# A two-stream fp32 transformer kernel: feed-forward norms by tokens, contexts of two head groups in one bank, exponents by head pair, new orders

## The chip, the cores and the metric

The kernel runs on one core of a Trainium2 chip, as one program. The metric is the time of an execution on the device, in microseconds. Before the change the median of three runs is 2144.49 us (2142.8 to 2147.58).

## What is computed

Sixteen sequences of 512 tokens and 128 channels, all fp32, each on its own. The reference, with the first norm, the modulation by a condition and the two layers:

```python
# per sequence: x (512, 128), condition c, six vectors from silu(c) @ wmod
# 1 attention with a latent: q = x@W_UQ, k = (x@W_DKV)@W_UK, v = (x@W_DKV)@W_UV
#   16 heads of 8, causal softmax(q k^T / sqrt(8)) v, then @ W_O, gated, added to x
# 2 twice, with weights of layer l:
h = shift_token(x)                 # the second half of the channels comes from the token before
q, k, v = split(h @ wqkv)          # 8 heads of 64
q, k = l2norm(q) * q_scale, l2norm(k) * k_scale
q, k = rotary_xpos(q, k)
o = local_attention(q, k, v)       # windows of 64, each sees itself and the one before
x = x + o @ wo
h = shift_token(x)
h = (h - mean(h)) / sqrt(var(h) + 1e-5) * g + b     # over the 128 channels
a, gate = split(h @ w1 + b1)       # 2 x 341
x = x + (a * gelu(gate)) @ w2 + b2
```

The mean and the variance of the last norm are what the change calls the norm of a feed-forward part.

## The kernel before, in words

Two streams of sequences run beside each other: even sequences in buffers of stream 0, odd ones in those of stream 1, about half a sequence apart. Each sequence is a list of some 190 named steps (`steps()`); a step may have work on TensorE (`pe`), ScalarE (`act`), VectorE (`dve`), GpSimd (`pool`) and SyncE (`sp`, transfers). The order in which each engine takes the steps is written out by hand: `PLACES` is the order inside a stream, `TURNS` says bit by bit which stream is next, `merged()` joins them. No engine deviates from its list, so an instruction that waits holds up everything behind it on its engine.

TensorE's results go to eight banks of PSUM, of 512 fp32 columns each. `FIRST_BANKS` gives each result its bank (some take two); `Banks.take` makes TensorE wait until the readers of the bank's last result are done. `FILLS` puts filler matmuls (constants, 128x512 bf16) into a bank ahead of a result.

The steps of the causal attention: `max` (scores for the row maxima, reduced on VectorE), `rows1` (maxima turned), `score` (scores turned, exponent on ScalarE), `ctx` (context of a group of four heads, 32 small products, L564), `turn` (four transposes, then VectorE divides by the sum), `join`, `out` (product with W_O and the residual; its vector step is L967).

The steps of a layer: `qkv` and `v` (products of 512 columns, L594, L595, L604), the squares on ScalarE (L788), `rotate` on VectorE (cosine product L982, two sine products L989, sum of squares L991) and GpSimd (their sum L1091), `norm` (inverse length, ScalarE; GpSimd scales the keys L1101), `qheads` and `kheads` (transposes). Then by head pair p: `wscore` (scores of 128x1024 into two banks, L636; VectorE's row maxima L1000 and their product with the inverse query lengths L1006), `wexp` (ScalarE, eight calls of 128x128 with own scale, bias and sum, L815), `share` (reciprocals of the sums L1021, GpSimd scales L1108), `pturn` (four transposes per head, copied by VectorE, L1014), `wctx` (context, L658). Then `wout` (product with wo, L667; residual L1026) and the feed-forward part: `center` (product of the centring matrix with the channels-by-tokens h, L491; squares on ScalarE L736), `spread` (product of the averaging matrix with the squares, so that each channel's row holds the variance of each token, L496; logarithm and exponent over 128x512, L739 and L741), `scale` (VectorE multiplies, L928), `hid` (L678, L681, the gelu L832, product L1033), `down` (L687, L1037), `final` (four transposes, the last vector step L1043, and the transfer out). Transposes have one line for all, L430; the filler matmuls are L234.

## Time and profile before

| | |
|---|---|
| median of 3 runs | 2144.49 us |
| profiled execution, first to last instruction | 2140.7 us |
| TensorE busy | 1949.1 us, 91% |
| ScalarE busy | 1607.3 us, 75% |
| VectorE busy | 1559.3 us, 73% |
| GpSimd busy | 862.1 us, 40% |
| instructions | 56,185 |

The busy shares are means over the span. In the view by slices TensorE stands at 9 tenths in all slices but the first three and the last two. Since the streams repeat, one period (from the last vector step of a sequence to that of the next) shows nearly all.

### The profile page before, as it was taken

How to read it: one execution, taken by the hardware profiler on the slowest of the kernel's cores; microseconds unless marked ns; L12 is line 12 of the kernel's file. 1: busy time of each engine (PE TensorE's matmuls, PEld its weight loads, DVE VectorE, ACT ScalarE, POOL GpSimd, SP SyncE). 2: the span in 40 equal slices, each digit the busy share in tenths (PEclk: the TensorE clock that was granted, in tenths of full speed). 3: DMA queues.
4: the chain of work that ended last, by engine and by line, in shares of the span. 5: the costliest groups of instructions: out<-in, count | busy, mean ns of one | idle time of the engine just before them, and what ended most of it. 6: DMA issues, size and time to landing. Idle time of an engine off the chain costs nothing.

```text
span 2140.7 us, 56185 instructions
## 1 busy us (share of the span) xinstructions
PE 1949.1 (91%) x22308; PEld 1117.7 (52%) x22308; DVE 1559.3 (73%) x2671; ACT 1607.3 (75%) x3975; POOL 862.1 (40%) x826
## 2 busy tenths in 40 slices
PE   6789999999999999999999999999999999999987
PEld 3344545555454655545555554655545455554644
DVE  3476787877778777787877778687777877777753
ACT  1567878787887878777787887878688787877755
POOL 2043616245351624526163361625435162452522
PEclk8999999999999999999999999999999999999999
DMA  4110201213030120202112030120203012030100
GB/s 137 29 32 16 61 7 36 41 24 58 7 68 9 39 43 24 58 7 57 21 32 51 24 58 7 38 39 24 58 7 70 13 36 42 24 53 7 36 6 23
DMA packets 63110, 76.19 MB, mean 36 GB/s; under 512 B 10630, under 2 KB 57856, under 8 KB 60800
## 3 DMA queue, kind: packets, MB, share of 16 engines
q1 hardware_dynamic: 62852, 72.60, 16.1%
q8 instruction: 180, 2.95, 0.6%
q14 instruction: 78, 0.64, 0.1%
HBM read 9.14 MB, written 4.19 MB: 6 GB/s over the span
## 4 chain that ended last, share of the span: by engine, by line
PE 56%; ACT 23%; DVE 12%; issue 5%; SPq 2%; DMA 1%; POOL 1%; DVEq 0%; ACTq 0%; POOLq 0%
PE ps L430 10%; ACT pr L815 6%; PE ps L667 5%; PE ps L564 5%; ACT pr L777 5%; PE ps L594 4%; PE ps L595 4%; PE ps L604 4%; PE ps L658 3%; PE ps L449 3%; ACT pr L788 3%; DVE wm L1000 3%; PE ps L678 2%; PE ps L445 2%; PE ps L687 2%
## 5 line engine op out<-in xcount | busy, mean ns | idle before, releaser
L1091 POOL TENSOR_TENSOR pr<-pr 128x1024 f32<-128x1024 f32 x128 | 302.2, 2361 | 739.7 <-DVE pr L989 739.7
L815 ACT ACTIVATE pr<-ps,wb,inv 128x128 f32<-128x128 f32 x768 | 340.8, 481 | 24.6 <-DVE wb L1006 24.2
L777 ACT ACTIVATE pr<-ps 128x1024 f32<-128x1024 f32 x320 | 314.4, 1028 | 42.5 <-PE ps L449 42.0
L1108 POOL TENSOR_TENSOR pr<-pr,shares 128x512 f32<-128x512 f32 x192 | 199.9, 1048 | 314.0 <-DVE shares L1021 314.0
L947 DVE TENSOR_REDUCE nm<-ps 128x2 f32<-128x256 f32 (+2 forms) x384 | 314.5, 861 | 13.0 <-PE ps L449 11.9
L430 PE MATMUL ps<-cf,pr 128*128 128x128 f32 x1792 | 259.7, 282 | 31.1 <-POOL pr L1108 22.5
L430 PEld LDWEIGHTS ps<-cf,pr 128*128 128x128 f32 x1792 | 200.9, 142 | 124.4 <-issue 55.0
L982 DVE TENSOR_TENSOR pr<-ps,rot 128x1024 f32<-128x1024 f32 x128 | 156.2, 1221 | 120.1 <-ACT pr L788 97.7
L788 ACT ACTIVATE pr<-ps 128x1024 f32<-128x1024 f32 x128 | 131.2, 1025 | 104.6 <-PE ps L595 66.2
L445 PE MATMUL ps<-cb 64*64 64x256 bf16 (+1 forms) x2560 | 175.3, 263 | 30.1 <-ACT pr L777 14.4
L1014 DVE COPY pr<-ps 128x512 f32<-128x512 f32 x256 | 170.1, 679 | 15.2 <-PE ps L430 13.7
L815 ACT ACTIVATION_READ_ACCUMULATOR pr<-ps,wb,inv 128x1 f32 x768 | 175.9, 229 | 0.0
L1000 DVE TENSOR_REDUCE wm<-ps 128x8 f32<-128x1024 f32 x128 | 155.6, 1216 | 25.9 <-PE ps L636 25.9
L989 DVE TENSOR_TENSOR pr<-ps,rot 128x512 f32<-128x512 f32 x256 | 163.7, 681 | 0.0
L445 PEld LDWEIGHTS ps<-cb 64*64 64x64 bf16 x2560 | 72.4, 104 | 168.5 <-issue 82.7
L564 PE MATMUL ps<-pr,V 128*16 128x512 f32 (+3 forms) x2048 | 152.4, 439 | 6.3 <-ACT pr L777 6.3
L991 DVE TENSOR_REDUCE scr<-pr 128x16 f32<-128x1024 f32 x128 | 154.8, 1209 | 0.0
L594 PE MATMUL ps<-Wqkv,hs 128*128 128x512 f32 x256 | 137.1, 617 | 7.4 <-ACT pr L777 3.6
L1101 POOL TENSOR_TENSOR pr<-pr,inv 128x512 f32<-128x512 f32 x128 | 133.4, 1042 | 19.3 <-POOL inv L1096 0.4
L636 PE MATMUL ps<-Kf,Q 64*64 64x128 f32 (+1 forms) x4096 | 137.0, 263 | 0.0
L658 PE MATMUL ps<-pr 128*64 128x64 f32 x2048 | 133.4, 229 | 2.1 <-DVE pr L1014 1.9
L636 PEld LDWEIGHTS ps<-Kf,Q 64*64 64x64 f32 x4096 | 129.7, 133 | 4.5
(158 smaller groups left out, 4040.0 us busy)
## 6 DMA issues: line engine op xcount, KB each, us to landing
pr<-V SPq DMA_DIRECT2D x32, 512.0 KB, 4.5
queries<-early SPq DMA_DIRECT2D x224, 64.0 KB
keys<-early SPq DMA_DIRECT2D x224, 64.0 KB
pr<-V SPq DMA_DIRECT2D x32, 384.0 KB, 6.6
xn<-in_L_attn_x SPq DMA_DIRECT2D x16, 256.0 KB, 4.5
out<-hT SPq DMA_DIRECT2D x16, 256.0 KB, 2.2
queries<-mT SPq DMA_DIRECT2D x128, 4.0 KB
Wqkv<-in_L_ffn_wqkv SPq DMA_DIRECT2D x1, 1536.0 KB
```

The lines of the kernel that those rows point to most:

```text
L430: mm = pe.transpose(dst[:, t * P:(t + 1) * P], src(t), ident)
L445: pe.matmul(dst, identb[here, here], mask, start=True, stop=False, skip_group_check=True)
L564: mm = pe.matmul(bank[32 * j:32 * j + 16, kt * P:T], V1[s][:, kt, 4 * g + j, :], pr[s][:, j, OFF[kt]:OFF[kt] + T - kt * P], start=(kt == 0 ...
L594: pe.matmul(bank[:, 0:T], lhs, Wqkv[:, l, 0:T], start=True, stop=True)
L636: mm = pe.matmul(bank[D2 * half:D2 * half + D2, r * T + (t + 1) * P - wd:r * T + (t + 1) * P], Q2[s][rows, p, q0:q0 + D2], K2[s][rows, p, ...
L658: mm = pe.matmul(bank[D2 * r:D2 * r + D2, q0:q0 + D2], val[s][:, t, 2 * p + r, :], PT[s][:, (2 * n + r) % 3, q0:q0 + D2], start=True, stop ...
L777: act.activation(dst, src, ACT.Exp, scale=SC1).then_inc(ex_r[s], 1)
L815: ins = act.activation(P2[s][2 * (p % 3) + r][:, o:o + P], bank[:, r * T + o:r * T + o + P], ACT.Exp, scale=inv[s][:, t, h:h + 1], bias=wb ...
L947: ins = dve.tensor_reduce(nm[s][:, qt, h:h + 2], src[:, :, o:o + (qt + 1) * P], AX_X, ALU.max, negate=True)
L1000: dve.tensor_reduce(dst, src, AX_X, ALU.max, negate=True).then_inc(wm_r[s], 1)
L1091: pool.tensor_tensor(t1[s][t % 3], t1[s][t % 3], t2[s], ALU.add).then_inc(sum_r[s], 1)
L1108: pool.tensor_tensor(part, part, share, ALU.mult).then_inc(part_r[s], 1)
```

## The change

- The norm of a feed-forward part goes by tokens. `center` is four transposes of h in place of the product with the centring matrix; VectorE takes batch statistics of each 128 tokens (mean and variance of 128 channels), `spread` is two calls of ScalarE on 128x4 in place of two on 128x512 and has no product, `scale` multiplies by the inverse deviation and transposes back (four transposes and a copy on ScalarE). W1 is centred ahead, as before.
- `ctx`: the values are laid out 32 columns wide per head, with zeros, so that two groups of four heads add into one bank; one copy and one `turn` serve both.
- `qkv` and `rotate` go by halves, queries and keys, each in one bank. GpSimd now scales the queries too, before their transposes.
- `wexp` is one exponent over 128x1024 per head pair, in place in SBUF: VectorE first subtracts the maxima (from PSUM), and sums the exponents afterwards. The reciprocals go by pair.
- `pturn` is copied by ScalarE in place of VectorE.
- TensorE waits for data before it waits for the bank, but ahead of fillers. Some vector waits that others cover are gone.
- All orders, banks and fillers are new: each stream has a list of its own, the pattern repeats every two sequences; 2,390 banks are given out in place of 2,326, and 308 fillers in place of 161. Between the outputs of sequences 0 and 13 they are 108 (65 before); 104 (56) stand before the first, 96 (40) after that of sequence 13. The first step of sequence 1's causal attention comes after the first head pair of sequence 0's layer 0; before, it came after that layer's first rotations.

The diff, cut to its core (indentation cut too; the orders, turns and banks are strings of digits and lists of step numbers and are left out):

```diff
-    out = [("keep",), ("values",)] + units[0] + [("rows1", 0)] + units[1] + [("rows1", 1)]
+    out = [("stats", 0), ("plain", 0), ("load",), ("proj", 0), ("proj", 1), ("keep",), ("values",)] + units[0] + [("rows1", 0)] + units[1] + [("rows1", 1)]
...
-            if j == 0 and g:
-    out += [("turn", g - 1)]
+            if j == 0 and g == 2:
+    out += [("turn", 0)]
...
-            out += [("qkv", l, t), ("rotate", l, t), ("v", l, t)] * (t < NT) + [("norm", l, t - 1)] * (1 <= t <= NT)
+            out += [("qkv", l, t, 0), ("rotate", l, t, 0), ("qkv", l, t, 1), ("rotate", l, t, 1), ("v", l, t)] * (t < NT) + [("norm", l, t - 1)] * (1 <= t <= NT)
...
-            out += [("wscore", l, p), ("wexp", l, p, 0), ("share", l, p, 0), ("wexp", l, p, 1), ("share", l, p, 1)] * (p < NP2)
+            out += [("wscore", l, p), ("wexp", l, p), ("share", l, p)] * (p < NP2)
...
 FILLS = {
-    2: 2, 7: 20, 17: 7, 69: 10, 70: 3, 74: 2, 77: 6, 103: 1, 187: 4, 188: 1, 332: 4, 333: 1, 477: 4, 478: 1, 622: 4,
-    623: 1, 767: 4, 768: 1, 912: 4, 913: 1, 1057: 4, 1058: 1, 1202: 4, 1203: 1, 1347: 4, 1348: 1, 1492: 4, 1493: 1,
-    1637: 4, 1638: 1, 1782: 4, 1783: 1, 1927: 4, 1928: 1, 2072: 4, 2073: 1, 2217: 4, 2218: 1, 2250: 10, 2254: 2,
-    2257: 1, 2283: 1, 2290: 1, 2292: 3, 2293: 2, 2296: 1, 2304: 2, 2305: 1, 2307: 3, 2308: 1, 2309: 1, 2316: 1,
-    2318: 4, 2325: 1,
+    7: 20, 59: 2, 63: 13, 64: 2, 69: 13, 79: 11, 80: 1, 83: 1, 84: 1, 85: 2, 89: 19, 90: 1, 92: 4, 97: 3, 187: 5,
...
-        for sem, value in dict.fromkeys(self.last[k] + self.last[k + count - 1]):
-            pe.wait_ge(sem, value)
+        self.due = list(dict.fromkeys(self.last[k] + self.last[k + count - 1]))
...
+        if FILLS.get(i, 0):
+            self.free(pe)
+            for _ in range(FILLS[i]):
+    self.fill(pe, self.view(k, 1))
         return self.view(k, count), self.full[k]
+
+    def free(self, pe):
+        for sem, value in self.due:
+            pe.wait_ge(sem, value)
+        self.due = []
 
...
-        V1 = [a[:, 0:NT * H1 * 16].rearrange("p (t h c) -> p t h c", t=NT, c=16) for a in V]
+        V1 = [a[:, :].rearrange("p (u q j c) -> p u q j c", q=2, j=4, c=32) for a in V]
...
-        P2 = [[a[:, i * T:(i + 1) * T] for i in range(4)] + [c[:, :], d[:, 4 * T:5 * T]] for a, c, d in zip(flat, y, scr)]
+        P2 = [[a[:, 0:2 * T], a[:, 2 * T:4 * T], c[:, 4 * T:6 * T]] for a, c in zip(flat, scr)]
...
-            bank, full = banks.take(pe, (b, "xc", n), [sq_r.at(b, n - 1)])
+            bank, full = banks.take(pe, (b, "xc", n), [yt_r.at(b, n - 1)])
             pe.wait_ge(*hsa_r.at(b, 2 * (n - 2) + 2))
             pe.wait_ge(*hsp_r.at(b, 2 * (n - 2) + 2))
-            pe.matmul(bank, centre, hs[s][:, :], start=True, stop=True).then_inc(full, 1)
-        elif kind == "spread":
+            banks.free(pe)
+            transposes(bank, lambda t: hs[s][:, t * P:(t + 1) * P]).then_inc(full, 1)
+        elif kind == "scale":
             n, = a
-            bank, full = banks.take(pe, (b, "var", n), [rs_r.at(b, 2 * (n - 1) - 1)])
-            pe.wait_ge(*sq_r.at(b, n - 1))
-            pe.matmul(bank, mean, sq[s], start=True, stop=True).then_inc(full, 1)
...
             for kt in range(NT):
                 for j in range(4):
-                    mm = pe.matmul(bank[32 * j:32 * j + 16, kt * P:T], V1[s][:, kt, 4 * g + j, :],
+                    mm = pe.matmul(bank[32 * j:32 * j + 32, kt * P:T], V1[s][:, 2 * kt + g // 2, g % 2, j, :],
                                    pr[s][:, j, OFF[kt]:OFF[kt] + T - kt * P],
-                                   start=(kt == 0), stop=(kt == NT - 1))
-            mm.then_inc(full, 1)
+                                   start=(kt == 0 and g % 2 == 0), stop=(kt == NT - 1), skip_group_check=True)
+            mm.then_inc(full if g % 2 else cx_r[s], 1)
...
+            bank, full = banks.take(pe, (b, "qkv", l, t, j), [t_r.at(b, 3 * (2 * (n - 1) + j + 1))])
...
-            pe.matmul(bank[:, 0:T], lhs, Wqkv[:, l, 0:T], start=True, stop=True)
-            pe.matmul(bank[:, T:2 * T], lhs, Wqkv[:, l, T:2 * T], start=True, stop=True).then_inc(full, 1)
+            banks.free(pe)
+            pe.matmul(bank, lhs, Wqkv[:, l, j * T:(j + 1) * T], start=True, stop=True).then_inc(full, 1)
...
-                pe.wait_ge(*sum_r.at(b, n))
+                pe.wait_ge(*rot_r.at(b, 2 * n - 1))
...
-            bank, full = banks.take(pe, (b, "wscore", l, p), [we_r.at(b, 2 * n + 2)], 2)
+            bank, full = banks.take(pe, (b, "wscore", l, p), [wd_r.at(b, n + 1)], 2)
...
-            act.activation(sq[s], banks.wait(act, (b, "xc", n)), ACT.Square).then_inc(sq_r[s], 1)
         elif kind == "spread":
             n, = a
-            act.activation(rs[s], banks.wait(act, (b, "var", n)), ACT.Ln, bias=eps[:, 0:1]).then_inc(rs_r[s], 1)
+            act.wait_ge(*va_r.at(b, n - 1))
+            act.activation(dev[1][s][:, :], mv[1][s][:, :, 1], ACT.Ln, bias=eps[:, 0:1]).then_inc(rs_r[s], 1)
             act.wait_ge(*rs_r.at(b, 2 * (n - 1) - 1))
-            act.activation(rs[s], rs[s], ACT.Exp, scale=-0.5).then_inc(rs_r[s], 1)
+            act.activation(dev[1][s][:, :], dev[1][s][:, :], ACT.Exp, scale=-0.5).then_inc(rs_r[s], 1)
+        elif kind == "scale":
+            n, = a
+            act.activation(y[s][:, :], banks.wait(act, (b, "yT", n)), ACT.Copy).then_inc(y_r[s], 1)
...
-            for t in range(NT):
-                ins = act.activation(V1[s][:, t, :, 0:D1], src[:, t], ACT.Copy)
+            act.wait_ge(*vone_r.at(b, 1))
+            for q in range(2):
+                ins = act.activation(V1[s][:, :, q, :, 16 * q:16 * q + D1], src[:, :, q], ACT.Copy)
...
+            l, p = a
+            act.wait_ge(*wd_r.at(b, NP2 * l + p + 1))
+            act.activation(P2[s][p % 3], P2[s][p % 3], ACT.Exp).then_inc(we_r[s], 1)
+        elif kind == "pturn":
             l, p, r = a
             n = NP2 * l + p
-            act.wait_ge(*wb_r.at(b, n + 1))
-            bank = banks.wait(act, (b, "wscore", l, p))
-            if p >= 3:
-                banks.wait(act, (b, "pturn", l, p - 3, r))
-            for t in range(NT):
-                o, h = t * P, 2 * p + r
-                ins = act.activation(P2[s][2 * (p % 3) + r][:, o:o + P], bank[:, r * T + o:r * T + o + P], ACT.Exp,
-                                     scale=inv[s][:, t, h:h + 1], bias=wb2[s][:, t, h:h + 1],
-                                     accum_out=sums[s][:, t, h:h + 1])
-            ins.then_inc(we_r[s], 1)
+            bank = banks.wait(act, (b, "pturn", l, p, r))
+            if 2 * p + r >= 3:
+                banks.wait(act, (b, "pv", l, (2 * p + r - 3) // 2))
+            act.activation(PT[s][:, (2 * n + r) % 3, :], bank, ACT.Copy).then_inc(pt_r[s], 1)
         elif kind == "wctx":
...
+                bank = banks.held((b, "xc", n)).rearrange("p (t c) -> p t c", c=P)
                 dve.wait_ge(*rs_r.at(b, 2 * (n - 1)))
-                dve.tensor_tensor(y[s][:, :], hs[s][:, :], rs[s], ALU.mult).then_inc(y_r[s], 1)
+                dve.tensor_tensor(yt[s].rearrange("p (t c) -> p t c", c=P), bank,
+                                  dev[1][s][:, :].unsqueeze(2).broadcast_to([P, NT, P]), ALU.mult).then_inc(yt_r[s], 1)
+        elif kind == "center":
+            n, = a
+            bank = banks.wait(dve, (b, "xc", n))
+            for t in range(NT):
+                dve.bn_stats(bn[1][s][:, t, :], bank[:, t * P:(t + 1) * P]).then_inc(bl_r[s], 1)
+            dve.wait_ge(*bl_r.at(b, NT * (n - 1)))
+            for t in range(NT):
+                ins = dve.bn_aggr(mv[1][s][:, t, :], bn[1][s][:, t, :])
+            ins.then_inc(va_r[s], 1)
         elif kind == "proj":
...
+            own = slice(j * T, (j + 1) * T)
+            qk = bank.rearrange("p (h d) -> p h d", h=H2)
+            cos = rot[:, l, 0, t, j, :].unsqueeze(1).broadcast_to([P, H2, D2])
+            dve.tensor_tensor(t1[s][i][:, own].rearrange("p (h d) -> p h d", h=H2), qk, cos, ALU.mult).then_inc(t_r[s], 1)
...
+                sin = rot[:, l, 1, t, j, o:o + 32].unsqueeze(1).broadcast_to([P, H2, 32])
+                dve.tensor_tensor(t2[s][:, own].rearrange("p (h d) -> p h d", h=H2)[:, :, o:o + 32],
+                                  qk[:, :, q:q + 32], sin, ALU.mult).then_inc(t_r[s], 1)
+            if j == 1:
+                dve.tensor_reduce(nrm[s][:, i, 0, :], sqk[s].rearrange("p (h d) -> p h d", d=D2), AX_X,
+                                  ALU.add).then_inc(ss_r[s], 1)
...
+            low = wm2[s][:, 2 * p:2 * p + 2, :].rearrange("p r t -> p (r t)")
+            dve.tensor_reduce(low, src.rearrange("p (j n) -> p j n", n=P), AX_X, ALU.max, negate=True).then_inc(wm_r[s], 1)
             dve.wait_ge(*wm_r.at(b, n + 1))
-            if p == 0:
-                dve.wait_ge(*inv_r.at(b, NT * (l + 1)))
+            if p >= 3:
+                for r in range(2):
+                    banks.wait(dve, (b, "pturn", l, p - 3, r))
+            dve.tensor_tensor(P2[s][p % 3].rearrange("p (j n) -> p j n", n=P), src.rearrange("p (j n) -> p j n", n=P),
+                              low.unsqueeze(2).broadcast_to([P, 2 * NT, P]), ALU.add).then_inc(wd_r[s], 1)
+        elif kind == "share":
+            l, p = a
+            n = NP2 * l + p
+            total = sums[s][:, 2 * p:2 * p + 2, :].rearrange("p r t -> p (r t)")
+            dve.wait_ge(*we_r.at(b, n + 1))
             if n >= NP2 or b >= S2:
-                dve.wait_ge(*we_r.at(b, 2 * (n - NP2 + 1)))
-            dve.tensor_tensor(wb2[s][:, :, 2 * p:2 * p + 2], wm2[s][:, :, 2 * p:2 * p + 2],
-                              inv[s][:, :, 2 * p:2 * p + 2], ALU.mult).then_inc(wb_r[s], 1)
-        elif kind == "pturn":
-            l, p, r = a
-            n = NP2 * l + p
...
-            pool.memset(V1[s][:, :, :, D1:16], 0.0).then_inc(vone_r[s], 1)
+            pool.memset(V[s][:, :], 0.0).then_inc(vone_r[s], 1)
             pool.wait_ge(*vone_r.at(b, 1))
-            pool.memset(V1[s][:, :, :, D1:D1 + 1], 1.0).then_inc(vone_r[s], 1)
+            for q in range(2):
+                pool.memset(V1[s][:, :, q, :, 16 * q + D1:16 * q + D1 + 1], 1.0).then_inc(vone_r[s], 1)
...
-            v = t1[s][t % 3][:, T:2 * T].rearrange("p (h d) -> p h d", d=D2)
-            one = inv[s][:, t, H2:2 * H2].unsqueeze(2).broadcast_to([P, H2, D2])
-            pool.tensor_tensor(v, v, one, ALU.mult).then_inc(rot_r[s], 1)
+            for j in range(2):
+                v = t1[s][t % 3][:, j * T:(j + 1) * T].rearrange("p (h d) -> p h d", d=D2)
+                one = inv[s][:, t, j * H2:(j + 1) * H2].unsqueeze(2).broadcast_to([P, H2, D2])
+                pool.tensor_tensor(v, v, one, ALU.mult).then_inc(rot_r[s], 1)
...
```

## Rows read from the trace of the kernel before

**Rows 1.** The page, busy time, share of the span and instructions, by engine.

```profile
PE 1949.1 (91%) x22308; PEld 1117.7 (52%) x22308; DVE 1559.3 (73%) x2671; ACT 1607.3 (75%) x3975; POOL 862.1 (40%) x826
```

**Rows 2.** Timeline of VectorE, last step of sequences 0, 3, 4, 13, 15: start, duration (us).

```profile
285.04 0.69 DVE L1043 TENSOR_TENSOR hT<-ps,x 128x512 f32<-128x512 f32 x1 [0.17 <-PE ps L430]
...
665.25 0.69 DVE L1043 TENSOR_TENSOR hT<-ps,x 128x512 f32<-128x512 f32 x1 [0.17 <-PE ps L430]
792.44 0.69 DVE L1043 TENSOR_TENSOR hT<-ps,x 128x512 f32<-128x512 f32 x1 [0.17 <-PE ps L430]
...
1933.91 0.69 DVE L1043 TENSOR_TENSOR hT<-ps,x 128x512 f32<-128x512 f32 x1 [0.18 <-PE ps L430]
...
2137.36 0.69 DVE L1043 TENSOR_TENSOR hT<-ps,x 128x512 f32<-128x512 f32 x1 [0.75 <-PE ps L430]
```

**Rows 3.** Busy time by stretch; columns as the first line says, x counts instructions.

```profile
core 0: us, PE busy (x) PEld busy (x) DVE busy (x) ACT busy (x) POOL busy (x), PEclk, DMA share, GB/s
919.30:1046.05 126.75, 118.28 (x1394) 68.14 (x1397) 96.81 (x166) 100.41 (x249) 53.80 (x51) 1.00 0.18 35
712.00:728.00 16.00, 14.45 (x217) 11.23 (x217) 12.87 (x33) 13.54 (x50) 6.06 (x7) 0.89 0.26 60
648.00:664.00 16.00, 14.70 (x230) 9.15 (x229) 14.66 (x25) 7.83 (x28) 3.14 (x3) 1.00 0.01 3
1009.30:1025.30 16.00, 13.86 (x171) 8.29 (x171) 9.02 (x17) 14.06 (x44) 6.16 (x9) 1.00 0.67 119
977.30:993.30 16.00, 13.70 (x136) 8.78 (x138) 13.90 (x24) 14.17 (x47) 9.21 (x9) 1.00 0.03 7
0.00:285.04 285.04, 231.75 (x2586) 132.74 (x2590) 181.19 (x331) 164.19 (x406) 94.28 (x103) 0.95 0.21 52
2063.05:2137.40 74.35, 56.26 (x422) 29.60 (x420) 33.12 (x53) 36.78 (x103) 22.93 (x20) 0.93 0.07 17
```

**Rows 4.** Waits of TensorE from 919.30 to 1046.05, longest first: us, times, longest.

```profile
PE ps L678 <- DVE y L928: 1.5, 1, 1.5
```

**Rows 5.** Timeline of TensorE: start, duration of the group (us), instructions.

```profile
907.03 0.66 PE L430 MATMUL ps<-cf,pr 128*128 128x128 f32 x4
907.62 0.30 PE L445 MATMUL ps<-cb 64*64 64x256 bf16 x4
...
917.73 1.10 PE L496 MATMUL ps<-scr,cf 128*128 128x512 f32 x2
918.67 0.60 PE L430 MATMUL ps<-cf,hT 128*128 128x128 f32 x4
...
974.16 1.04 PE L234 MATMUL ps<-cf 128*128 128x512 bf16 x4
```

**Rows 6.** Instruction groups by form: busy us, mean ns | idle before, releaser.

```profile
L815 ACT ACTIVATE pr<-ps,wb,inv 128x128 f32<-128x128 f32 x768 | 340.8, 481 | 24.6 <-DVE wb L1006 24.2
L815 ACT ACTIVATION_READ_ACCUMULATOR pr<-ps,wb,inv 128x1 f32 x768 | 175.9, 229 | 0.0
L788 ACT ACTIVATE pr<-ps 128x1024 f32<-128x1024 f32 x128 | 131.2, 1025 | 104.6 <-PE ps L595 66.2 <-DVE scr L991 36.3
L791 ACT ACTIVATE V<-ps 128x512 f32<-128x512 f32 x128 | 74.5, 595 | 15.6 <-PE ps L604 15.6
L1014 DVE COPY pr<-ps 128x512 f32<-128x512 f32 x256 | 170.1, 679 | 15.2 <-PE ps L430 13.7
L989 DVE TENSOR_TENSOR pr<-ps,rot 128x512 f32<-128x512 f32 x256 | 163.7, 681 | 0.0
L982 DVE TENSOR_TENSOR pr<-ps,rot 128x1024 f32<-128x1024 f32 x128 | 156.2, 1221 | 120.1 <-ACT pr L788 97.7 <-issue 22.5
L991 DVE TENSOR_REDUCE scr<-pr 128x16 f32<-128x1024 f32 x128 | 154.8, 1209 | 0.0
L1006 DVE TENSOR_TENSOR wb<-wm,inv 128x8 f32<-128x8 f32 x128 | 46.9, 367 | 4.4
L864 DVE BATCH_NORM_STATS2 scr<-x 128x6 f32<-128x128 f32 x64 | 14.0, 281 | 1.5
L1101 POOL TENSOR_TENSOR pr<-pr,inv 128x512 f32<-128x512 f32 x128 | 133.4, 1042 | 19.3 <-POOL inv L1096 0.4
```

361 lines of the change are left out of this document (203 added, 158 removed), and 62 rows, old and new, of tables (FILLS, PLACES).

## The prediction

> **What bounds the kernel now.** I read the busy times first, then the times of the last vector step of each sequence, then busy time by stretch, then the single waits inside one period. TensorE is busy 91% of the span, no other engine over 75% [rows 1]. The work is periodic: the last vector step of sequence 0 starts at 285.04 us and that of sequence 13 at 1933.91, so a sequence leaves every 1648.87 / 13 = 126.84 us; the last one leaves at 2137.36 [rows 2]. So the time has three parts: 285 us up to the first output, 13 periods, and 203.5 us from output 13 to output 15. In one period of 126.75 us TensorE is busy 118.3, VectorE 96.8, ScalarE 100.4, GpSimd 53.8 [rows 3]. TensorE idles 8.4 us per period, in some fifteen waits, none longer than 1.5 us [rows 4]. The idle is not spread evenly. The stretches from 977.3 and from 1009.3 hold 2.3 and 2.1 us of it, and in both ScalarE is over 14 of 16 us busy; in the stretch from 648 it is VectorE that is nearly full (14.66 of 16) and TensorE idles 1.3 [rows 3]. So TensorE's own work is the bound, and what is lost beside it is lost where one of the two evicting engines is full for a while. The span is 2140.7 us and the median of the runs 2144.49, so 3.8 us lie outside the span; I work on the span and add them at the end.
>
> **TensorE's work, by period.** Both 512-column products of each feed-forward norm (centring and spreading the variance) become four transposes. The spreading product starts at 917.73 and the next instruction at 918.67, so it takes 0.94; four transposes start at 907.03 and the next step at 907.62, so they take 0.59 [rows 5]. Two products, two layers: 4 x 0.35 = 1.4 us less. The contexts of two head groups share a bank, so two of four "turn" steps go: 2 x 0.59 = 1.2 less. The context products themselves write 32 rows in place of 16 but stream the same columns; I cost that at nothing (no row has the 32-column weights of this form; bounds 0 and 1 us). The query and key products become two steps with a bank and a semaphore each; a step change costs up to the 0.09 us by which 0.94 exceeds the bare product, so 8 more of them cost 0 to 0.7, taken 0.4. Filler matmuls: the table has 161 before and 308 after, in the middle 5 per sequence before and 17 per two sequences, 8.5, after. Four fillers last 1.04 us together, so about 0.22 each beyond the first one's latency [rows 5]: 3.5 x 0.22 = 0.8 more. Sum: -1.4 - 1.2 + 0.4 + 0.8 = -1.4 us per period, between -2.2 and -0.1.
>
> **ScalarE's work, by period.** The head-pair exponent was eight calls on 128x128 with eight reads of the accumulator: 340.8 + 175.9 us for 768 of the 1,024 calls [rows 6], so 689 us in all, 43.1 per sequence. It becomes eight calls on 128x1024, and such a call takes 1.03 [rows 6]: 8.2. The copies of the turned shares come over from VectorE: 16 x 0.60 = 9.6 (a 512-column copy takes 595 ns [rows 6]). The squares are halved in size: 16 x 0.60 for 8 x 1.03, +1.3. The norm loses three 512-column passes per layer and gains one copy and two tiny calls, -1.5; two context copies go, -1.2. Sum: -34.9 + 9.6 + 1.3 - 1.5 - 1.2 = -26.7, so ScalarE falls from 100.4 to about 74 of each period.
>
> **VectorE's work, by period.** Added: eight subtractions of the maximum at 1.22 (the form of the cosine product, PSUM with a broadcast [rows 6]), 9.8; eight sums over 1,024 at 1.21 [rows 6], 9.7; eight batch statistics at 14.0 / 64 = 0.22 [rows 6] and eight aggregations at about 0.1, 2.5. The rotation goes by halves: by the two sizes, 681 ns for 512 and 1221 for 1,024 [rows 6], an element costs 1.055 ns, so 256 cost about 411 ns (an estimate from these two), and a token tile goes from 1.22 + 2 x 0.68 to 2 x (0.68 + 2 x 0.41), +0.4, 3.3 for eight. Removed: the share copies, 170.1 / 16 = 10.6, the biases, 46.9 / 16 = 2.9 [rows 6], half of the reciprocals and turns, 1.7. Sum: 9.8 + 9.7 + 2.5 + 3.3 - 10.6 - 2.9 - 1.7 = +10.1, so VectorE rises from 96.8 to 107.
>
> **GpSimd and the queues.** GpSimd also scales the queries now, 8 x 1.04 = 8.3 [rows 6], and clears a four times larger V: 54 becomes about 64 of a period. The query transposes now wait for that scaling, 1.04 us later than the sum they waited for; the key transposes waited for it already. Cover: products of the other sequence stand between them in TensorE's new order. If it is gone, 8 x 1.04 = 8 us per sequence; taken 0, since GpSimd is the emptiest engine [rows 1]. ScalarE's copy of the attention values now waits for the clearing; behind it on ScalarE are context copies and maxima, but the clearing is issued on GpSimd ahead of the last shares of the other sequence, so taken 0, bounds 0 and 1.6 per period. On SyncE the load of the next input is now ahead of the second half of the spreads, not behind; the transfer waits of TensorE are 0.3 us per period or less, taken 0, plus or minus 0.3. Semaphore waits for free banks now come after the waits for data; that alone moves no start.
>
> **What becomes of the waits.** Of the 4.4 us that TensorE idles in the two stretches where ScalarE is full, the new exponents take away the cause. I take 2.4 (0 to 4.4), since in the first of them VectorE is 13.9 of 16 busy too [rows 3] and receives work. For VectorE's extra 10 us I charge 1.0 of new waiting (0 to 5): most of it falls in stretches where VectorE is only 9 of 16 busy [rows 3], but it ends at a mean share of 107 / 123.9 = 86%. The score banks come free after the subtraction, 2.4 us after the product, in place of after eight exponents; this is in the 2.4. Period: 126.8 - 1.4 - 2.4 + 1.0 = 124.0, so 2.8 less, and 14 periods' worth (the 13 and the one before the last output) 39 us less.
>
> **The ends.** Up to the first output TensorE is busy 231.8 of 285.0 us, and in the last 74.35 us 56.3 [rows 3]; there one sequence runs alone and its chain sets the time. The fillers of the table stand where TensorE was meant to wait: 48 more up to the first output and 56 more after output 13. At 0.22 that is 23 us of standing, which partly replaces idle that is there already (53 and 18 us [rows 3]); I count half, +11. The work that is saved there, about 2 x 2.5, goes off: +6 in all (-5 to +25). Sum for the span: 2140.7 - 39 + 6 = 2107.7, and with the 3.8 outside 2111.5; I say 2111.
>
> **A rule of the notes against the change.** The granted clock is 1.00 in nearly every stretch, which is the 2.4 GHz level; only the stretch from 712 shows 0.89 [rows 3], so a part of it ran at 1.2 GHz, and the period around it (665.25 to 792.44) took 127.19 in place of 126.75 [rows 2, 3]: 0.44 us for one such dip. What TensorE did before it was a mixture of transposes and small head products. The Trainium skill (TensorE: Matmul & The Clock Gate, Part 4: PE-mode transpose) says that transposes don't count as activity for the clock the way products do. By that rule more dips follow where products turn into transposes; the trace neither bears it out nor excludes it. By the sum above nothing is charged; by the rule it is the last rival below.
>
> **The rivals.** (1) *All of ScalarE's waits go and VectorE's load hides*: 126.8 - 1.4 - 4.4 = 121.0 per period, 14 x -5.8 = -81, ends +4: 2068. For it: ScalarE and VectorE together fall from 197 to 181 per period. Against: VectorE is then 88% busy. (2) *Only TensorE's work counts*, each wait that leaves ScalarE comes back at VectorE: 14 x -1.4 = -20, ends +10: 2135. For it: the stretch from 648 already shows TensorE waiting beside a full VectorE. (3) *VectorE becomes the bound and the kernel is slower*: its 107 us per period can't be kept at more than 84% of the time, because maxima, rotations, subtractions and sums come in bunches: 107 / 0.84 = 127.4, 14 x 0.6 = 8, ends +20: 2173. It decides from the share where the gain is gone: with ends of +6 the period must stay below 126.8 - 0.4 = 126.4, so VectorE must reach 107 / 126.4 = 85%. It reaches 14.66 of 16, 92%, in its fullest stretch but 76% on the mean [rows 3]. (4) *The clock dips once or twice in each sequence*: forecast plus 14 to 28 dips at 0.44, 6 to 12: 2120. (5) That the change doesn't do what it says is not to be expected, as each edit is written out in instructions.
>
> **How the numbers follow.** Chances: forecast 0.43, (1) 0.20, (2) 0.13, (3) 0.17, (4) 0.07. The forecast's own range is 2090 to 2130. For 8 in 10 the range goes down to (1), 2066, and up over (2) into part of (3), 2152. A change under 0.2% (4.3 us, about what a measurement of this kernel can tell from no change) means 2140 to 2149: 0.08, from the upper part of (2) and the lower of (3). Slower by more: 0.14, nearly all from (3). Faster by more: 0.78.
>
> **What would show it.** Distance of two successive last vector steps: 124.0 (121 by rival 1, 126 by 2, over 127 by 3). TensorE busy per period 117, VectorE 107, ScalarE 74, GpSimd 64. ScalarE is no releaser of TensorE's waits in the windowed attention any more; in their place stand subtraction and sum of VectorE. First output at about 290, last 75 to 90 us after the one before. Clock rows under 1.00 in most periods would speak for (4). I am wrong if GpSimd's query scaling is a leading releaser of the query transposes, or if VectorE's rotation by halves costs much over 3.0 us per tile.

## The result, and the profile after

The changed kernel takes 2194.32 us (median of four runs, 2191.69 to 2197.23) against 2144.77 for the kernel before: a ratio of 1.023, 95% interval 1.0218 to 1.0242. It is slower by 50 us; forecast were 34 us less.

The first rows of the page of the kernel after: busy time of each engine, and the chain of work that ended last (followed back from the last instruction, at each step to what released it), by engine. The last line is the same chain in the kernel before.

```profile
span 2191.6 us, 55172 instructions
PE 1965.6 (90%) x22455; PEld 1127.2 (51%) x22455; DVE 1730.8 (79%) x3023; ACT 1399.1 (64%) x2383; POOL 1027.8 (47%) x1098
...
PE 35%; DVE 27%; POOL 17%; ACT 13%; issue 5%; SPq 2%; DMA 1%; DVEq 0%; POOLq 0%; ACTq 0%
...
PE 56%; ACT 23%; DVE 12%; issue 5%; SPq 2%; DMA 1%; POOL 1%; DVEq 0%; ACTq 0%; POOLq 0%
```

TensorE's busy share is what it was [rows 1] and it still has the largest part of the chain, but 35% in place of 56%: VectorE and GpSimd, 44% of the chain together in place of 13%, hand each other the rotations, the norms and the shares. The longest single line of the chain is GpSimd's scaling of queries and keys by the inverse lengths (L1202), 7%.

The last vector step of sequences 0, 1, 2, 12, 13, 14 and 15 (start, duration), which answers to [rows 2]:

```profile
301.35 0.68 DVE L1141 TENSOR_TENSOR hT<-ps,x 128x512 f32<-128x512 f32 x1
...
439.04 0.68 DVE L1141 TENSOR_TENSOR hT<-ps,x 128x512 f32<-128x512 f32 x1
...
560.74 0.68 DVE L1141 TENSOR_TENSOR hT<-ps,x 128x512 f32<-128x512 f32 x1
...
1857.88 0.68 DVE L1141 TENSOR_TENSOR hT<-ps,x 128x512 f32<-128x512 f32 x1
...
1991.67 0.68 DVE L1141 TENSOR_TENSOR hT<-ps,x 128x512 f32<-128x512 f32 x1
...
2107.77 0.68 DVE L1141 TENSOR_TENSOR hT<-ps,x 128x512 f32<-128x512 f32 x1
...
2188.21 0.69 DVE L1141 TENSOR_TENSOR hT<-ps,x 128x512 f32<-128x512 f32 x1 [0.75 <-PE ps L481]
```

The loss stands in two places. The period is (1991.67 - 301.35) / 13 = 130.02 us in place of 126.84, which is 3.18 x 13 = 41.4 us. The first output comes 16.3 us later. From there to the end it is 7 us less (196.5 for 203.5). Sum: +50.7 on the span. One caution on the period: in the changed kernel and its edits the outputs alternate, 137.7 and 121.7 us apart at the start, and 13 distances hold seven long ones and six short. Over twelve the kernel after gives (1857.88 - 301.35) / 12 = 129.71, the kernel before 126.84 as over 13. So 2.9 is the loss per sequence, and the 7 us that the end seems to gain are this counting: from output 12 to the end it takes 333.7 us in place of 333.6.

Busy time by stretch, which answers to [rows 3]: up to the first output, two middle sequences, and the last 80 us (columns: stretch, its length, busy time and count of PE, PEld, DVE, ACT and POOL, granted clock, DMA share, GB/s).

```profile
0.00:301.35 301.35, 242.13 (x2695) 136.75 (x2696) 203.20 (x370) 148.02 (x258) 111.74 (x130) 0.93 0.23 49
...
819.84:1079.87 260.03, 238.35 (x2780) 138.00 (x2779) 214.88 (x375) 174.74 (x298) 128.23 (x136) 0.99 0.18 34
2107.77:2188.21 80.44, 68.36 (x491) 35.15 (x491) 40.57 (x68) 35.52 (x60) 27.35 (x28) 1.00 0.06 16
```

Per sequence TensorE is busy 119.2 us (117 was forecast), VectorE 107.4 (107), ScalarE 87.4 (74), GpSimd 64.1 (64). TensorE idles 10.8 us per sequence in place of 8.4, so most of the growth is waiting. The single waits of TensorE over the whole run (waiting line, its releaser: total, times, longest), first those that lead now, with the one for GpSimd's query and key scaling last:

```profile
PE ps L496 <- ACT pr L866: 32.2, 68, 0.9
PE ps L705 <- ACT scr L920: 22.9, 7, 3.6
PE ps L481 <- DVE scr L960: 15.3, 13, 1.6
PE ps L496 <- DMA keys<-early: 13.4, 1, 13.4
...
PE ps L481 <- POOL pr L1202: 10.8, 28, 0.7
```

and their counterparts in the kernel before, as far as there are any:

```profile
PE ps L445 <- ACT pr L777: 14.4, 34, 0.5
...
PE ps L627 <- ACT scr L832: 2.3, 3, 0.8
...
PE ps L445 <- DMA keys<-early: 1.6, 1, 1.6
PE ps L430 <- POOL pr L1101: 1.6, 3, 0.9
```

The first, for the exponents of the causal attention, more than doubled, but it is 32 to 33 us in the mended kernels below too, also in one (c2) that is as fast as the kernel before; no run prices it. The second comes once in two sequences, and the trace shows what is behind it. ScalarE's timeline in the layer-1 feed-forward of one of them (start, duration; L920 gelu, L795 and L797 the norm's Ln and Exp, L899 the head-pair exponents of the other sequence):

```profile
914.14 1.28 ACT L914 ACT_TABLE_LOAD   x1
915.43 0.69 ACT L920 ACTIVATE scr<-ps,B 128x512 f32<-128x512 f32 x1
916.14 1.28 ACT L795 ACT_TABLE_LOAD   x1
917.43 0.30 ACT L795 ACTIVATE dev<-mv,eps 128x4 f32<-128x4 f32 x1
917.75 1.28 ACT L797 ACT_TABLE_LOAD   x1
919.04 0.21 ACT L797 ACTIVATE dev<-dev 128x4 f32<-128x4 f32 x1
919.15 1.04 ACT L899 ACTIVATE pr<-pr 128x1024 f32<-128x1024 f32 x1
920.21 1.28 ACT L920 ACT_TABLE_LOAD   x1
921.50 0.69 ACT L920 ACTIVATE scr<-ps,B 128x512 f32<-128x512 f32 x1
```

and TensorE's at the same time:

```profile
918.08 1.02 PE L764 MATMUL ps<-scr,W 128*85 128x512 f32 x2
922.34 0.64 PE L705 MATMUL ps<-cb 64*64 64x512 bf16 x4 [3.24 <-ACT scr L920]
```

Three table loads and 1.6 us of other work stand between two gelus. TensorE has finished the layer's six gate and value products, and its next step, the score product of a head pair (`wscore`, L705), waits for a bank that the second gelu has to empty: TensorE is busy 0.36 of the 3.4 us from 919.3. The kernel before loads tables between gelus too, 28 times in all (around the causal exponents L777) and 93 times altogether, against 36 and 101 after; but there the loads don't come three in a row, and TensorE's waits of this kind are 2.3 us. It is the new order of ScalarE that bunches them. Then the third wait:

```profile
L960 DVE TENSOR_SCALAR scr<-x,mv,dev 128x128 f32<-128x128 f32 x64 | 39.2, 673 | 0.6 <-ACT dev L797 0.6
```

The same instruction took 336 ns before (64 of them 17.7 us); it now stands beside GpSimd's share products. The Trainium skill (SBUF — State Buffer, "SBUF: two separate sides") says that VectorE in a two-port mode and GpSimd take a shared port pair in turns, each for a whole instruction. The trace agrees: the mean of 673 hides 19 calls that no GpSimd instruction overlaps, 336 ns each, and 15 that lie wholly beside GpSimd's work, 1073 ns each, where one share product lasts 1051. The run below that moves the calls gives 351 ns.

### The profile page after: what moved, and what is told of

Its sections match the earlier page's. It is cut to its first block, busy times and chain, and to the rows that moved or that the text cites. A ratio compares the mean times of both kernels' runs of the same rounds, so it can differ in the third digit from the quotient of the medians.

```text
span 2191.6 us, 55172 instructions
## 1 busy us (share of the span) xinstructions
PE 1965.6 (90%) x22455; PEld 1127.2 (51%) x22455; DVE 1730.8 (79%) x3023; ACT 1399.1 (64%) x2383; POOL 1027.8 (47%) x1098
## 4 chain that ended last, share of the span: by engine, by line
PE 35%; DVE 27%; POOL 17%; ACT 13%; issue 5%; SPq 2%; DMA 1%; DVEq 0%; POOLq 0%; ACTq 0%
POOL pr L1202 7%; POOL pr L1191 6%; PE ps L481 6%; PE ps L635 5%; DVE nm L1046 5%; DVE wm L1100 5%; PE ps L669 4%; ACT pr L866 4%; PE ps L500 3%; DVE pr L1105 3%; DVE sums L1114 3%; PE ps L771 3%; PE ps L496 3%; PE ps L760 3%; PE ps L764 2%
## 5 line engine op out<-in xcount | busy, mean ns | idle before, releaser
L1191 POOL TENSOR_TENSOR pr<-pr 128x512 f32<-128x512 f32 x256 | 323.0, 1276 | 533.8 <-DVE pr L1088 532.3
L866 ACT ACTIVATE pr<-ps 128x1024 f32<-128x1024 f32 x320 | 309.6, 1025 | 109.9 <-PE ps L500 91.7
L1210 POOL TENSOR_TENSOR pr<-pr,shares 128x512 f32<-128x512 f32 x192 | 197.8, 1051 | 341.4 <-DVE shares L1118 341.4
L481 PE MATMUL ps<-cf,pr 128*128 128x128 f32 x1792 | 260.7, 282 | 39.0 <-POOL pr L1202 10.8
L1202 POOL TENSOR_TENSOR pr<-pr,inv 128x512 f32<-128x512 f32 x256 | 261.8, 1044 | 19.5 <-POOL inv L1196 0.9
L669 PE MATMUL ps<-Wqkv,hs 128*128 128x512 f32 x512 | 262.7, 617 | 7.0 <-DVE hs L1012 6.6
L1082 DVE TENSOR_TENSOR pr<-ps,rot 128x512 f32<-128x512 f32 x256 | 175.6, 686 | 99.2 <-ACT pr L878 84.2
L1088 DVE TENSOR_TENSOR pr<-ps,rot 128x256 f32<-128x256 f32 x512 | 191.1, 415 | 0.4 <-POOL pr L1191 0.2
L878 ACT ACTIVATE pr<-ps 128x512 f32<-128x512 f32 x256 | 148.1, 593 | 58.0 <-DVE scr L1091 32.2
L906 ACT ACTIVATE pr<-ps 128x512 f32<-128x512 f32 x256 | 144.1, 595 | 61.9 <-PE ps L481 44.8
L635 PE MATMUL ps<-pr,V 128*32 128x512 f32 (+3 forms) x2048 | 152.5, 439 | 3.7 <-ACT pr L866 3.6
L714 PE MATMUL ps<-Kf,Q 64*64 64x128 f32 (+1 forms) x4096 | 143.0, 272 | 0.0
L738 PEld LDWEIGHTS ps<-pr 128*64 128x64 f32 x2048 | 106.0, 138 | 69.1 <-ACT pr L906 47.7
L679 PE MATMUL ps<-Wqkv,hs 128*128 128x512 f32 x256 | 128.5, 600 | 0.5 <-ACT V L881 0.5
```

Source lines behind the costliest of these rows:

```text
L481: mm = pe.transpose(dst[:, t * P:(t + 1) * P], src(t), ident)
L635: mm = pe.matmul(bank[32 * j:32 * j + 32, kt * P:T], V1[s][:, 2 * kt + g // 2, g % 2, j, :], pr[s][:, j, OFF[kt]:OFF[kt] + T - kt * P], st ...
L669: pe.matmul(bank, lhs, Wqkv[:, l, j * T:(j + 1) * T], start=True, stop=True).then_inc(full, 1)
L714: mm = pe.matmul(bank[D2 * half:D2 * half + D2, r * T + (t + 1) * P - wd:r * T + (t + 1) * P], Q2[s][rows, p, q0:q0 + D2], K2[s][rows, p, ...
L738: mm = pe.matmul(bank[D2 * r:D2 * r + D2, q0:q0 + D2], val[s][:, t, 2 * p + r, :], PT[s][:, (2 * n + r) % 3, q0:q0 + D2], start=True, stop ...
L866: act.activation(dst, src, ACT.Exp, scale=SC1).then_inc(ex_r[s], 1)
```

## The experiments

Sixteen kernels, in five groups that each shared one chip and the runs of the kernel before (2144.6 to 2146.9). First output and period are read from the same vector step as above; busy times are per sequence, from a stretch of two middle sequences (for after, 958.16 to 1217.13). By the alternation above the periods of the edits of the kernel after are 0.3 to 0.7 too long; over twelve sequences t1 has 127.90, d1 127.62, c1 127.96, c2 126.85. The runs d1, g1, c2, a1, av1 and w1 leave work out, as said at each; they price a load, and are no kernels to use.

| run | us | ratio, interval | first output | period | VectorE | ScalarE |
|---|---|---|---|---|---|---|
| before | 2144.8 | | 285.0 | 126.84 | 96.7 | 100.4 |
| after | 2194.3 | 1.023 (1.0218-1.0242) | 301.4 | 130.02 | 107.4 | 87.5 |
| t1 act regrouped | 2176.0 | 1.0147 (1.013-1.0164) | 303.3 | 128.47 | 107.4 | 84.2 |
| p1 plain earlier | 2182.8 | 1.0185 (1.0167-1.0202) | 297.3 | 129.38 | 106.1 | 87.3 |
| g1 one query head | 2180.6 | 1.0165 (1.0146-1.0184) | 298.0 | 129.12 | 107.2 | 87.2 |
| d1 short sums | 2161.7 | 1.0075 (1.0054-1.0097) | 294.2 | 128.30 | 100.4 | 87.3 |
| k1 later keep | 2182.5 | 1.0172 (1.0156-1.0187) | 293.1 | 129.88 | 107.4 | 87.4 |
| f1 no middle fills | 2194.5 | 1.0234 (1.0218-1.025) | 301.1 | 130.07 | 107.2 | 87.3 |
| c1 three orders | 2164.7 | 1.0094 (1.0079-1.0109) | 294.1 | 128.48 | 106.0 | 84.2 |
| c2 orders, short sums | 2147.8 | 1.0006 (0.9993-1.002) | 292.2 | 127.28 | 99.1 | 84.2 |
| e5 exponents from bank | 2440.4 | 1.138 (1.1363-1.1397) | 310.0 | 147.03 | 87.0 | 100.9 |
| x1 sums with exponents | 2298.4 | 1.0717 (1.0701-1.0733) | 309.0 | 136.91 | 96.5 | 94.4 |
| r2 after, no maxima | 2133.5 | 0.9948 (0.9931-0.9966) | 291.6 | 126.77 | 87.7 | 86.3 |
| a1 ScalarE relieved | 2129.8 | 0.9931 (0.9916-0.9945) | 289.3 | 125.90 | 96.7 | 82.6 |
| av1 and VectorE loaded | 2200.0 | 1.0259 (1.0242-1.0276) | 296.0 | 129.67 | 103.8 | 82.8 |
| w1 loaded elsewhere | 2190.0 | 1.0209 (1.0192-1.0226) | 294.2 | 129.60 | 103.9 | 82.6 |
| b1 norms by tokens alone | 2298.6 | 1.0719 (1.0701-1.0737) | 298.6 | 136.54 | 98.7 | 99.1 |
| r1 before, no maxima | 2090.3 | 0.9742 (0.9725-0.9758) | 282.6 | 123.30 | 85.9 | 94.5 |

The runs from t1 to r2 are edits of the kernel after, those from a1 on of the kernel before.

**Orders of the changed kernel, one at a time.**

```diff
+# t1: keep ("stats",) and ("wexp",) from between the gelus of layer 1
+    order[first:last] = moved + rest    # first: (b, ("hid", 1, 0)), last: (b, ("hid", 1, 2))
...
+# p1: VectorE's ("plain", 1) right behind ("stats", 1)
+    order.insert(order.index((b, ("stats", 1))) + 1, (b, ("plain", 1)))
```

> The changed kernel with one edit to ScalarE's order: the logarithm, exponent and head-pair exponent that stand between the first and third gelu of layer 1 go ahead of the first gelu. Theory T (the new order of ScalarE costs what was lost): in the changed kernel ScalarE loads tables three times between two gelus, from 914.1 to 921.5 us, and TensorE waits 3.2 us there, once in two sequences (22.9 us in all); the run takes 2165 to 2175 us, a period of two sequences falls from 260 to about 257, and the 36 extra table loads fall to under 12. Theory V (VectorE's load of 107 us per period is the bound): TensorE's wait goes to VectorE instead, 2188 to 2196 us. Theory G (GpSimd's chain through the scaling of queries is the bound): also 2188 to 2196.

> The changed kernel with one edit to VectorE's order: the four normalising calls of the step plain 1 (line 960, 673 ns each on average here, 336 before) come right after their statistics, ahead of the sums of the other sequence's head pair 1, so that GpSimd is not scaling shares while they run. Theory T: the doubling comes from running beside GpSimd's two-input product, and it costs the order 1.2 us per sequence on the chain: the calls return to 0.35 us and the run takes 2172 to 2185 us. Theory V: the load of VectorE falls by 20 us in all, 2180 to 2192. If the doubling has another cause (the place of the output), the calls stay at 0.67 us and the time at 2190 to 2200.

t1 takes 18 us off, and it is in the period (-1.55); it ends 1 us above theory T's range and 12 below the two others'. Of the table loads, 32 + 32 for the gelus and one more are left; the kernel after has 36 beside these 65, the kernel before 28:

```profile
L928 ACT ACT_TABLE_LOAD x32 | 41.1, 1283 | 0.6
L937 ACT ACT_TABLE_LOAD x32 | 41.1, 1283 | 0.6
L943 ACT ACT_TABLE_LOAD x1 | 1.3, 1283 | 0.7 <-PEq L1347 0.7
```

p1 takes 11.5 off, which lies in the ranges of T and V alike; the instruction itself is back near its old duration, which is what T said and the other cause excluded. It is the row of after above (L960) under a new number:

```profile
L972 DVE TENSOR_SCALAR scr<-x,mv,dev 128x128 f32<-128x128 f32 x64 | 18.5, 351 | 9.6 <-ACT dev L809 9.6
```

```diff
+# k1: VectorE's ("keep",) of sequence 0 behind its last maximum
+    order.insert(order.index((0, ("max", 3, 4))) + 1, (0, ("keep",)))
```

> The changed kernel with one edit: VectorE's 'keep' of sequence 0, which waits for the late loads, behind the last maximum of that sequence. The first maximum product came at 52.7 us, 9.1 later than before. If the ramp carries this on to the end: 2185 (2182 to 2189). If the last loads or the first layer's own chain set the first output: 2190 to 2196.

2182.5 is the first case: the first output is 8.3 us earlier. Two waits show it, the first in the kernel after, the second, for the first key rows, in k1:

```profile
DVE rot L984 <- DMA B<-in_L_ffn_b: 14.6, 1, 14.6
```

```profile
PE ps L506 <- DMA keys<-early: 5.4, 1, 5.4
```

In the kernel after, VectorE waits 14.6 us for a late load ahead of what the spread needs, and TensorE 13.4 for the key rows behind it; with "keep" moved, 5.4. So half of the 16.3 us of the ramp is one step put ahead of a late load.

> The changed kernel with three edits of the orders at once: the norms' Ln/Exp and the head-pair exponents of the other sequence kept out from between the gelus (alone: 18 us less), the normalized tile of the attention input made right after its statistics (alone: 11.5 less), and VectorE's 'keep' of sequence 0, which waits for the late loads, moved behind the last maximum of that sequence (new: the first maximum product came 9 us later than before). If the three take away different waits, they add up: 2194 - 18 - 11.5 - 9 = 2155, range 2150 to 2161. If the first two remove the same waiting of TensorE, 2194 - 18 - 9 = 2167, range 2164 to 2172. If 'keep' wasn't on the path of the ramp, 4 to 9 more than either.

2164.7: the second case (2164 to 2172). The first output keeps k1's gain, but the period is 128.48, no better than t1's 128.47; t1 and p1 take away the same waiting. Together the moved steps are 30 us of the loss of 50, and 20 are left.

**Fillers and query scaling.**

```diff
+FILLS = {i: count for i, count in FILLS.items() if not 187 <= i <= 2161}    # f1
-one = inv[s][:, t, j * H2:(j + 1) * H2].unsqueeze(2).broadcast_to([P, H2, D2])
...
+some = H2 if j else 1                                                      # g1: one query head of eight
+one = inv[s][:, t, j * H2:j * H2 + some].unsqueeze(2).broadcast_to([P, some, D2])
```

> The changed kernel without the 119 filler products of the periodic middle (189 at the two ends stay). By the prediction a filler costs 0.22 us, 26 us in all. Theory 'fillers displace work': the time falls to about 2170 (2165 to 2178). Rival 'fillers stand in waits that are there anyway': within 5 us of 2194 if the clock stays, or slower, 2200 to 2220, if the granted clock dips more often without them.

> The changed kernel with GpSimd scaling one of eight query heads per token tile (the scaling of the other seven is left out): each call falls from 1.04 to about 0.2 us, GpSimd from 64 to about 57 us per period. Theory G: the chain through GpSimd (17% of the chain of waits, 0.8 us per tile in two layers) shortens by 0.8 x 4 = 3.3 us per layer where it is bare; bare in both layers 2110 to 2150 us, bare in one 2150 to 2175. Theory T or V: 2180 to 2195.

f1 takes the same time, but this doesn't mean that the fillers only stood in waits. From the first output to that of sequence 13, after and then f1:

```profile
301.35:1991.67 1690.32, 1549.70 (x18117) 895.86 (x18116) 1402.80 (x2442) 1140.15 (x1937) 833.53 (x884) 0.99 0.17 34
```

```profile
301.12:1992.03 1690.91, 1531.24 (x18009) 896.26 (x18008) 1401.93 (x2442) 1139.55 (x1937) 833.59 (x884) 0.98 0.17 34
```

The 108 fillers of this stretch were 32 us of TensorE's work. Without them TensorE is busy only 18.5 us less and idles 19.1 more. The other 13.5 is the same products running longer, and up to 12 of it is the clock: of this stretch 58 us are at 1.2 GHz in f1 and 34 in the kernel after (0.976 and 0.982 on the mean of the whole runs). So the fillers' price is nothing on balance, as a sum of two things: what they displace, and the clock, which falls more often without them. g1 takes 14 us off, 0.90 per period for the 5.9 us of GpSimd's time that it saves; 2180.6 lies at the fast end of the range of T and V, 6 us above G's.

**The load that moved from ScalarE to VectorE.** d1 and c2 shorten VectorE's sums of exponents; a1 takes work from ScalarE in the kernel before, av1 and w1 add work to VectorE there at two places.

```diff
-dve.tensor_reduce(total, P2[s][p % 3].rearrange("p (j n) -> p j n", n=P), AX_X, ALU.add)
+dve.tensor_reduce(total, P2[s][p % 3].rearrange("p (j n) -> p j n", n=P)[:, :, 56:72], AX_X, ALU.add)   # d1, c2
...
-    ins = act.activation(P2[s][2 * (p % 3) + r][:, o:o + P], bank[:, r * T + o:r * T + o + P], ACT.Exp,
-                         scale=inv[s][:, t, h:h + 1], bias=wb2[s][:, t, h:h + 1], accum_out=sums[s][:, t, h:h + 1])
+ins = act.activation(P2[s][2 * (p % 3) + r][:, :], bank[:, r * T:(r + 1) * T], ACT.Exp,
+                     scale=0.0, bias=eps[:, 0:1])                                                       # a1
...
+dve.tensor_reduce(again[s][:, :, :], src, AX_X, ALU.max, negate=True)    # av1: ahead of each maximum
...
+dve.tensor_reduce(again[s][:, :, :].rearrange("p r t -> p (r t)"), src, AX_X, ALU.add)   # w1: src = rot
```

> The changed kernel with VectorE's sums of the exponents cut from 128 to 16 columns per row (the sum over the other columns is left out), so each of 128 calls takes about 0.2 us in place of 1.21: VectorE's load falls from 107 to 99 us per period, near the 97 of the kernel before. Theory V: the waits of TensorE fall with it, 4 to 6 us per sequence, 2105 to 2135 us. Theory T: only the waits in the windowed attention shorten, 2165 to 2185 us. Theory G: 2175 to 2190.

> The kernel before with one term of the prediction alone: each head's exponents of the windowed attention are one call of 512 columns (0.60 us) in place of four calls of 128 with the row sums, pitch 0.435 each (left out: scale, maximum and sums, so the shares are all one). ScalarE loses 64 x 0.435 - 16 x 0.60 = 18 us per sequence, nothing else changes. The prediction booked 2.4 us per period for ScalarE's relief: 2145 - 14 x 2.4 = 2111 (2100 to 2122). Rival: TensorE was not held up by ScalarE's fullness but by latencies between engines that stay: 2135 to 2147.

> The same with the other term added: VectorE takes each maximum of the window scores twice, 8 x 1.24 = 9.9 us more per sequence, the net of what the change gives it, at the place where it subtracts. The prediction charged 1.0 us per period for that: 14 us above the run with ScalarE relieved alone (5 to 20). Rival 'VectorE's time stands in TensorE's way': 2.5 or more per period, 35 to 80 us above it, so that the exchange of ScalarE's time for VectorE's gives a kernel slower than the one before, 2145 to 2190.

> The kernel before with ScalarE relieved (2129.8 us) and with as much work added to VectorE as in the run of doubled maxima (2200.0), but off the path: eight sums over 1,024 constants, 1.21 us each, 9.7 per sequence, each behind the reciprocal of a head pair, read by nobody. Theory 'a queue in order': an instruction on VectorE delays whatever stands behind it, wherever it stands, so nearly the same price, 2180 to 2205. Rival 'latency of the chain': the price comes from the place, between score product and exponents, and is mostly gone here, 2130 to 2150.

Two middle sequences of a1, of av1 and of w1, in the columns of the stretches above:

```profile
919.05:1170.97 251.92, 236.04 (x2780) 136.16 (x2781) 193.41 (x330) 165.23 (x273) 107.65 (x102) 1.00 0.18 35
```

```profile
944.64:1204.24 259.60, 240.92 (x2780) 140.33 (x2780) 207.61 (x346) 165.66 (x273) 107.66 (x102) 0.97 0.17 34
```

```profile
941.90:1200.87 258.97, 237.00 (x2780) 136.12 (x2782) 207.82 (x347) 165.17 (x273) 107.69 (x102) 1.00 0.18 34
```

The same loads in three lines. ScalarE (a1) loses 17.8 us of each sequence and the period falls by only 0.94: neither theory's number, between them. VectorE then gets 7.1 us of busy time more (the added calls are 9.7, but the small product behind each maximum gets shorter, from 386 to 183 ns, and the rows overlap a little more) and the period rises by 3.77, or 3.70 where nobody reads what the added work writes. So VectorE's microsecond costs 0.5 at either place: it is the queue in order, not the place in the chain. TensorE's waits in w1 show it: behind the added sums stand VectorE's copies of the turned shares (L1014), and they lead now; the same two rows were 16.2 and 1.9 us in the kernel before.

```profile
PE ps L432 <- DVE pr L1014: 30.1, 32, 1.4
PE ps L660 <- DVE pr L1014: 26.6, 33, 1.1
```

Not all of the 0.5 is waiting. Over 13 periods TensorE's idle time grows by 26 us in av1 and 37 in w1, and its busy time, for the same products, by 23 and 11; its granted clock fell from 0.988 in a1 to 0.970 in av1 and 0.982 in w1, which is a part of it. So a wait costs its own time and, where the clock falls behind it, some more.

A kernel with this exchange of load alone, 2200.0, is as slow as the changed one. d1 looks at it from the other side: 7.0 us less on VectorE, period -1.72 (0.25 for each), 33 us off. That is between theory V (2105 to 2135) and theory T (2165 to 2185): VectorE's load matters, and it is not the whole.

> The changed kernel with the three edits of the orders (2164.7 us) and VectorE's sums of the exponents over 16 of 128 columns (left out: seven eighths of each sum; 33 us less in the changed kernel by itself). If VectorE's load is what is left of the loss, the two add up and it falls below the kernel before: 2165 - 33 = 2132 (2125 to 2140). If both had removed the same waiting, 2150 or more.

c2 lies between the two cases, 17 us below c1 and level with the kernel before. VectorE's load is a part of what the orders left, but with the orders mended a microsecond of it is worth less, 1.20 / 6.9 = 0.17.

**The exchange undone inside the changed kernel.** Both keep all else of the change and c1's orders.

```diff
-act.activation(P2[s][p % 3], P2[s][p % 3], ACT.Exp).then_inc(we_r[s], 1)
+ins = act.activation(own, own, ACT.Exp, accum_out=sums[s][:, 2 * p + r, t:t + 1])        # x1, eight times
...
+ins = act.activation(P2[s][p % 3][:, o:o + P], bank[:, o:o + P], ACT.Exp,                # e5, eight times
+                     bias=wm2[s][:, 2 * p + r, t:t + 1], accum_out=sums[s][:, 2 * p + r, t:t + 1])
```

> The changed kernel with the three edits of the orders (2164.7 us) and its head-pair exponents undone: no subtraction and no sum on VectorE, eight calls of 128 columns on ScalarE straight from the bank with the negated maximum as bias and the row sums taken along, as the kernel before has them. All else of the change stays (norms by tokens, query scaling on GpSimd, share copies on ScalarE, banks); in ScalarE's order the exponents of pairs 2 and 3 go ahead of what would block them. VectorE 8 x (1.22 + 1.21) = 19.4 us less per sequence, ScalarE 64 x 0.435 - 8 x 1.06 = 19.4 more. By the prices of the runs so far, VectorE's microsecond at 0.30 (the short sums) to 0.50 (the doubled maxima) and ScalarE's at 0.06: 14 x 19.4 x (-0.30 + 0.06) = -65 to -120, so 2045 to 2100. Rival: ScalarE, at 107 us of a period, becomes the late engine and the score banks wait for eight calls: 2150 or more.

> The changed kernel with the three edits of the orders (2164.7 us) and one exchange of load back: the subtraction stays on VectorE, so that the banks come free as planned, but the exponents are eight calls of 128 columns that take their row sums along, in place of one of 1,024 and VectorE's sum. VectorE 8 x 1.21 = 9.7 us less per sequence, ScalarE 64 x 0.435 - 8 x 1.06 = 19.4 more, to about 104. By the prices of the runs so far (VectorE's microsecond 0.30 to 0.50, ScalarE's 0.06): 2164.7 - 14 x 9.7 x (0.30 to 0.50) + 14 x 19.4 x 0.06 = 2113 to 2140, faster than the kernel before. Rival: ScalarE's price rises as it fills (the copies of the shares stand behind the eight calls), so that nothing is gained: 2155 to 2200.

Both missed by far; e5 is in its rival's open range (2150 or more), x1 98 us beyond its rival's. In x1 ScalarE is no fuller than it was before the change, and yet 8.4 us per period are lost. Among the waits of TensorE that lead now are those for the copies of the shares (L946), which stand in ScalarE's queue behind the eight calls:

```profile
PE ps L313 <- ACT pr L946: 36.8, 15, 3.1
...
PE ps L774 <- ACT pr L946: 27.1, 19, 2.3
```

The likely reading is that an order written for one call of 1.06 us doesn't hold for eight with a pitch of 0.29, or of 0.34 from the banks in e5, where I also moved exponents. It is not shown, as no run has the eight calls in an order made for them. What the two runs do show is that they can't be used to price the exponents.

**One part of the change alone in the kernel before.**

```diff
+order.insert(max(at, order.index((b, ("spread", n))) + 1), (b, ("back", n)))    # PE: transposes back ahead of "hid"
...
+order.insert(out + 1, (b, ("center", n)))                                       # DVE: statistics behind "wout"
```

> The kernel before with one part of the change alone: the feed-forward norms by tokens (transposes in, batch statistics and scaling on VectorE, transposes back, one copy on ScalarE). The prediction gave TensorE 1.4 us less per period for it, VectorE 2.5 more, ScalarE 1.5 less. If only TensorE's work counts: 2145 - 14 x 1.4 = 2125 (2120 to 2130). With VectorE's microsecond at 0.45, as the loaded runs have it: 2145 - 20 + 14 x 2.5 x 0.45 = 2141 (2132 to 2152). Above 2155 if the longer chain of the norm (two engines more between the output product and the gate product) holds up TensorE.

```profile
PE ps L456 <- DVE scr L962: 49.3, 17, 3.3
PE ps L471 <- DVE scr L962: 43.2, 14, 3.1
```

Far above 2155. TensorE waits for the scaled tile in both layers of nearly each sequence, 92.5 / 31 = 3.0 us each time, 5.8 per sequence, and the clock of the middle stretch is 0.94. The token form is a longer chain (TensorE, VectorE, ScalarE, VectorE, TensorE, ScalarE), and at the old places nothing covers it. The period is 9.7 us longer: 6.0 of it is TensorE's idle time, 3.7 is more busy time, at this lower clock. So this part can't be judged without its order; that its 1.4 us reach the period wasn't shown by any run.

**Without the maxima.** Queries and keys are normalized, so an unmasked score is at most 8 times the learned scales, and the softmax needs no shift as long as these are near one, as they are here.

```diff
-dve.tensor_reduce(dst, src, AX_X, ALU.max, negate=True).then_inc(wm_r[s], 1)
...
-                         scale=inv[s][:, t, h:h + 1], bias=wb2[s][:, t, h:h + 1],
+                         scale=inv[s][:, t, h:h + 1],                             # r1
...
-act.activation(P2[s][p % 3], P2[s][p % 3], ACT.Exp).then_inc(we_r[s], 1)
+act.activation(P2[s][p % 3], bank, ACT.Exp).then_inc(we_r[s], 1)                 # r2
```

> The kernel before without the maxima of the window scores: queries and keys are normalized, so an unmasked score is at most 8 times the learned scales, and the exponents need no shift; the result is the reference's. VectorE loses 8 x 1.24 + 2.9 = 12.8 us per sequence, ScalarE waits for the product and not for VectorE. If VectorE's microsecond is worth the same in both directions (0.30 to 0.50): 2145 - 14 x 12.8 x (0.30 to 0.50) = 2055 to 2091. If a relief saturates, as ScalarE's did (0.06): 2125 to 2137, since TensorE at 118.3 of 126.8 has 8.4 us of idle per period to give back and most of it is waiting in the single chains of the norms and the rotations.

> The changed kernel with the three edits of the orders (2164.7 us) and without the maxima and the subtraction: one call of 1,024 columns on ScalarE straight from the banks, for the same reason with the reference's result; the sum stays on VectorE. VectorE 8 x (1.22 + 1.24) = 19.7 us less per sequence, ScalarE the same, a step fewer in the chain. By the price of the short sums (0.30) 2165 - 83 = 2082, range 2060 to 2110. If the orders of exponents and share copies, which were written for the longer chain, hold it up as they did the exponents from the bank: 2160 or more.

Two middle sequences of r1:

```profile
899.89:1146.79 246.90, 234.81 (x2778) 136.50 (x2781) 171.76 (x299) 188.93 (x497) 108.13 (x102) 1.00 0.18 36
```

r1 is the fastest kernel of the study, 2090.3 us, 2.6% under the kernel before. VectorE's 10.9 us less per sequence give 3.54 per period: 0.33 us each, and no saturation such as ScalarE's. The 0.33 is not VectorE's alone: ScalarE is busy 5.9 us less as well, and its exponents no longer wait for the maxima. The wait that [rows 4] has once per sequence at 1.5 us, here over the whole run of the kernel before,

```profile
PE ps L678 <- DVE y L928: 21.1, 15, 1.6
```

is down to 0.9 us. r2 gains 31 us for 18.3 us of VectorE's time, where its range asked for 55 to 105; whether there too an order that was written for a longer chain stands in the way was not tested.

## Why the prediction was wrong

**The bound: half right.** TensorE's work was the largest part, but not alone what sets the period: in the chain of the kernel before it has 56%, ScalarE 23% and VectorE 12%, and in one stretch VectorE is 14.66 of 16 full [rows 3].

**TensorE's work: the saving was mis-sized.** Forecast was -1.4 per period, from -2.2 for the edits and +0.8 for fillers; measured from first output to output 13 it is +0.7 (118.5 to 119.2). The fillers of this stretch, before and after (busy time and count):

```profile
285.04:1933.91 1648.87, 18.40 (x65) 5.28 (x65) 1.00 0.17 35
```

```profile
301.35:1991.67 1690.32, 31.98 (x108) 8.42 (x108) 0.99 0.17 34
```

That is 1.4 us per sequence before and 2.5 after: +1.0, near the 0.8. Without them 117.08 becomes 116.75, so 0.3 is what is left of the 2.2 that the edits should save. Up to 1.0 more is hidden by the lower clock (2.1 us more of each period at 1.2 GHz); the rest isn't there. On balance the fillers cost nothing (f1).

**ScalarE's work: wrong by 13 us.** I added the rows of the exponent call and of its accumulator read [rows 6]; they overlap, and a pair of them has a pitch of 0.435 us, so the old form cost 28 per sequence and not 43.1. ScalarE fell by 13, not 26.7. It changed little, since the relief is worth little: 0.05 us for each, by a1.

**VectorE and GpSimd: right, 107 and 64.** The rotation by halves costs 415 ns for 256 columns (411 was estimated).

**What becomes of the waits: this step failed.** It booked -2.4 per period for ScalarE and +1.0 for VectorE's extra 10 us. Measured in the kernel before: -0.94 for 17.8 us of ScalarE, and 0.51 to 0.53 per microsecond of VectorE. At these prices the change's 13 us of ScalarE give 0.7 and its 10.7 us of VectorE cost 5.6. In the changed kernel itself VectorE's microsecond is worth less, 0.25 (d1) or, with orders mended, 0.17 (c2): 2.7 or 1.8. So the balance of this step, booked at -1.4, is between +1.1 and +4.9, with the sign the other way. The measured +3.18 lies inside; the runs don't fix it closer. The reason given, that most of VectorE's load falls where it is only 9 of 16 busy, doesn't hold: three of the eight maxima of a period stand in that very stretch [rows 3], av1 doubles them, and its microsecond costs as much as that of w1, whose work stands at other places.

**The moves of steps: they weren't in the sum, and were 30 us.** I charged the new orders at nothing: table loads bunched between gelus (18 us), and "keep" ahead of a late load (12 us). Each step that is moved on a queue in order is a change of its own. VectorE's neighbour on GpSimd wasn't in the sum either; it is 11.5 us by itself and nothing more once the table loads are moved. The query scaling was taken at 0 (bounds 0 and 8); 5.9 of its 8.3 us are worth 0.9 per period. This was the prediction's own sign of being wrong: TensorE's wait for the scaling went from 1.6 to 10.8 us in the whole run, and the scaling is the longest line of the chain (both rows hold the keys' scaling too, which was there before).

**The miss in numbers, an estimate.** From 2111 to 2194 it is 83 us. The moved steps are 30 of them (c1). ScalarE's relief, booked at 2.4 and worth 0.7, is 14 x 1.7 = 24. The last 29 lie in VectorE's load, the query scaling and TensorE's work, and no run divides them.

**The third rival came nearest, partly by luck.** It had the kernel slower, at 2173, by VectorE's load alone; without the moved steps the kernel takes 2164.7, and shorter sums on VectorE bring that to 2147.8. So the direction was VectorE's. But VectorE is no bound in its sense: its mean share is 107.4 / 130 = 83% and its part of the chain 27%, below TensorE's 35%. The 21 us from 2173 to 2194, and some more, are the moves, for which it had no row.

**The ends: the sum right by luck.** +6 was charged, +9.3 came, as +16.3 up to the first output and -7 behind, which is the alternation of the outputs (over twelve periods it is +16.4). The +6 was made of fillers and saved work; half of the 16.3 is "keep", which wasn't in it.

**The clock: a small part, and behind the waits.** It is granted 0.982 in place of 0.989, which is 78 us at the lower of its two levels, 1.2 GHz, in place of 48. If TensorE had been busy in all of the 30 more, they cost at most 15 of the 50 us. f1 doesn't exclude this, as its fillers and its clock changed together. In the middle, the fourth rival's ground, it is 34 us in place of 7. Each of the nine stretches at 1.2 GHz there stands behind idle time of TensorE, at least 1.6 of the 4 us ahead of it, as this one behind the wait for the gelu:

```profile
919.00:922.00 3.00, 0.10 (x1) 0.00 (x0) 2.01 (x3) 2.96 (x5) 0.24 (x1) 0.97 0.07 16
922.00:924.00 2.00, 1.66 (x30) 1.53 (x34) 0.75 (x1) 0.19 (x1) 1.80 (x2) 0.50 0.03 8
```

TensorE is all but idle for 3 us, and then at half speed for two. The rule on transposes that was set against the change wasn't tested. In seven of the nine no transpose ran in those 4 us, so these drops need no such rule; in the two others, and in both of the kernel before, idle time and transposes stand together, and no run separates them.

**What stays open.** With orders mended (c1) a sequence takes 127.96 over twelve against 126.84, 1.1 more, and 9 us of the ramp are left; seven of VectorE's microseconds are worth 17 us there. How the rest divides between VectorE's remaining load, GpSimd's longer turns and banks that are held longer was not told apart. The parts of the change were not judged in orders made for them: b1, x1, e5 and perhaps r2 say more about the order than about the part.

## What to carry to other kernels

Where several engines work through queues in order, an added microsecond on an engine that isn't the bound is not free: on VectorE it cost 0.5 us in this kernel at either of two places, and a removed one gave 0.33 there and 0.1 to 0.25 in the changed kernel, while one removed from ScalarE gave 0.05. Measure both prices before a load is moved from the one to the other. An order or bank plan belongs to the durations it was made for: judge a part together with its order, and read in each moved step what table, load or port it now stands beside. And before a load is moved between engines, ask whether it is needed at all: leaving the maxima out was worth more than any exchange.

## What the runs showed of the hardware

- A table load on ScalarE takes 1.283 us in each of the 101 records of the kernel after. An Ln and the Exp behind it need one each where they follow a gelu (L795 and L797 above, 6 times); the other 26 such pairs, which follow the load that the kernel itself asks for behind the last gelu (L923), need none.
- A tensor_scalar of 128x128 in SBUF took 336 ns on VectorE with GpSimd elsewhere and 1073 wholly beside GpSimd's share products of 1051 (673 on the mean of all 64), and 351 on the mean when moved away.
- The accumulator read of an activation overlaps with the call beside it: 481 and 229 ns by the rows [rows 6], 435 ns of pitch for both together.
- Without 119 filler products, 108 of them between the outputs of sequences 0 and 13, the granted clock was 0.976 in place of 0.982, 58 us of that stretch were at 1.2 GHz in place of 34, and the products that were left kept TensorE busy 13.5 us longer there.
